# Turning round the order of heads and channels on the partitions of a linear attention stage

## What is computed

```
ms = concatenate([qkv, agg], axis=1).reshape(B, 64, 24, 4096)      # 64 heads: 8 q, 8 k, 8 v channels each
q, k = relu(q), relu(k);  v = v with a column of ones
kv  = einsum('bgnd,bgne->bgde', k, v)                               # per head 8 x 9
out = einsum('bgnd,bgde->bgne', q, kv)
out = out[..., :-1] / (out[..., -1:] + 1e-15)
x   = x + conv1x1(out, w_proj)                                      # 512 -> 256 channels
```

## Time and profile before

| | |
|---|---|
| three runs | 8548.59, 8554.9, 8555.37 us; median 8554.9 |
| the profiled execution | 8550.38 us, its span 8548.7 us |
| TensorE busy over the span | 93% |
| VectorE, GpSimd, ScalarE busy | 66%, 52%, 42% |
| linear attention, first load to last store | 2558.87 to about 3308 us |
| TensorE's granted clock, mean | 0.979 of 2.4 GHz |

### The profile page before, as it was taken

How to read it: one execution, slowest core, us unless ns; L and a number is a source line. 1 busy time by engine, 2 the same in 40 slices (tenths; PEclk the granted TensorE clock), 3 DMA queues, 4 the chain that set the end, 5 groups by cost and what they waited for, 6 DMA issues and landing times. The chain is left out here.

```text
span 8548.7 us, 155575 instructions
## 1 busy us (share of the span) xinstructions
PE 7935.8 (93%) x55794; PEld 6737.4 (79%) x55794; DVE 5657.7 (66%) x8857; ACT 3583.2 (42%) x7004; POOL 4479.1 (52%) x1996
## 2 busy tenths in 40 slices
PE   5999998899996996999999999999999999969999
PEld 4777776799995774888888888888888888857777
DVE  5666664344442556998888888989988898851110
ACT  3555555333322332555445454455554555531110
POOL 3555551033330001777778777777777877841111
PEclk9999999999998998999999999999999999989999
DMA  3111115755555541000000000000000000022221
GB/s 136 56 62 57 62 51 188 243 144 142 145 138 209 205 179 54 13 18 13 17 12 13 18 13 17 12 13 18 18 13 11 13 18 18 6 72 61 63 57 53
DMA packets 613257, 567.80 MB, mean 66 GB/s; under 512 B 464085, under 2 KB 481621, under 8 KB 610374
## 3 DMA queue, kind: packets, MB, share of 16 engines
q1 hardware_dynamic: 578246, 455.11, 18.2%
q0 software_dynamic: 33856, 96.69, 3.1%
q10 hardware_dynamic: 576, 8.39, 0.2%
HBM read 366.33 MB, written 193.76 MB: 66 GB/s over the span
## 5 line engine op out<-in xcount | busy, mean ns | idle before, releaser
L1824 POOL TENSOR_TENSOR e_ev<-e_se,e_v 128x2048 f32<-128x2048 f32 (+1 forms) x896 | 3307.9, 3713 | 940.6 <-ACT e_se L1787 940.6
L1787 ACT ACTIVATE e_se<-e_stage 128x512 f32<-128x512 f32 x3136 | 1870.1, 598 | 2074.4 <-PE e_stage L1654 2044.4
L1915 DVE SCALAR_TENSOR_TENSOR e_stage<-e_k,e_rl,e_qp 128x512 f32<-128x512 f32 x3136 | 2299.1, 746 | 330.8 <-ACT e_se L1787 296.7
L1661 PE MATMUL e_pv_sum<-e_ident,e_ev 128*128 128x128 f32 x12544 | 1872.5, 273 | 35.7 <-issue 35.2
L1661 PE MATMUL e_pe_sum<-e_ident,e_se 128*128 128x128 f32 x12544 | 1879.7, 272 | 12.4 <-ACT e_se L1787 12.2
L1661 PEld LDWEIGHTS e_pe_sum<-e_ident,e_se 128*128 128x128 f32 x12544 | 1557.8, 140 | 241.5 <-ACT e_se L1787 16.8
L1661 PEld LDWEIGHTS e_pv_sum<-e_ident,e_ev 128*128 128x128 f32 x12544 | 1485.5, 141 | 266.2 <-issue 213.6
L1654 PE MATMUL e_stage<-e_top,e_minus 128*128 128x512 f32 x3136 | 1509.5, 481 | 51.8 <-DVE e_stage L1915 47.2
L403 POOL TENSOR_TENSOR a_pr<-a_pr,a_rden 128x480 f32<-128x480 f32 x512 | 495.1, 990 | 587.4 <-DVE a_rden L636 587.4
L903 POOL DMA_DIRECT2D agg<-c_ot x384 | 334.6, 874 | 887.5 <-DVE c_ot L962 776.7
L1654 PEld LDWEIGHTS e_stage<-e_top,e_minus 128*128 128x128 f32 x3136 | 595.8, 190 | 108.3 <-DVE e_stage L1915 81.2
(11 more groups left out here) (160 smaller groups left out, 11911.3 us busy)
## 6 DMA issues: line engine op xcount, KB each, us to landing
qkv<-b_ot SPq DMA_DIRECT2D x120, 512.0 KB, 5.9
c_xt<-qkv SPq DMA_DIRECT2D x384, 160.0 KB, 3.8
agg<-c_ot POOLq DMA_DIRECT2D x384, 160.0 KB, 2.5
a_xb<-in_x SPq DMA_DIRECT2D x24, 768.0 KB, 5.0
a_xr<-in_x SPq DMA_DIRECT2D x32, 512.0 KB, 3.8
x<-a_xr SPq DMA_DIRECT2D x32, 512.0 KB, 2.8
b_xc<-x SPq DMA_DIRECT2D x32, 512.0 KB, 6.1
d_xr<-x POOLq DMA_DIRECT2D x32, 512.0 KB, 7.8
```

The costliest lines, as they stand in the source:

```text
L1661: last = nc.tensor.matmul(acc[:, c * PART:(c + 1) * PART], lhsT=src[:, c * PART:(c + 1) * PART], rhs=ident[:], is_transpose=True, start=j ...
L1787: nc.scalar.activation(se[(t * K2 + o) % NSE][:, i], stage[:, bank_of(t, j), :], ACT.Exp)\
L1824: nc.gpsimd.tensor_tensor(split(ev[(t * NG2 + g) % NEV][:, 0:size]), split(se[(t * K2 + o) % NSE][:, i:i + size]), window(v[h], h, u, o, i ...
L1915: nc.vector.scalar_tensor_tensor(rows(stage[:, bank_of(t, j), :]), win, rl[:, h, o:o + 1], rows(qp[:]), ALU.add, ALU.mult).then_inc(multip ...
```

## The change

The DRAM pattern of the loads gets the head as its outer and the channel as its inner dimension, so that partition p holds channel p % 8 of head p // 8. Mask, mask column, denominators and products follow; the rows of the projection weights need no reordering any more. The patterns on the chip's side of the loads stay, 128 partitions by the run's pixels, and so do sizes, counts and waits.

```
-            return bass.AP(tensor=one.tensor, offset=one.offset, ap=[[BLKPX, G8], [3 * GPX, TG], [1, (last - first) * WW]])
+            return bass.AP(tensor=one.tensor, offset=one.offset, ap=[[3 * GPX, TG], [BLKPX, G8], [1, (last - first) * WW]])
...
-                nc.vector.tensor_scalar(kvm[b % 2][:, st, PART:ONE], hm[:, 0:TG], pkv[:, PART:PART + 1], None, ALU.mult)\
+                nc.vector.tensor_scalar(kvm[b % 2][:, st, PART:ONE], hm[:].rearrange("p (g i) -> p g i", i=G8)[:, :, 0], pkv[:, PART:PART + 1], None, ALU.mult)\
...
-                    last = nc.vector.tensor_tensor(attp[i % 2][:, sub].rearrange("p s (i g) -> p s i g", g=TG),
-                                                   ratios[:, h, :, 0:PART].rearrange("p s (i g) -> p s i g", g=TG),
-                                                   den[i % 2][:, sub].rearrange("p s (o g) -> p s o g", o=1)
-                                                   .to_broadcast([PART, SPB, G8, TG]), ALU.mult)
+                    last = nc.vector.tensor_tensor(attp[i % 2][:, sub].rearrange("p s (g i) -> p s g i", g=TG),
+                                                   ratios[:, h, :, 0:PART].rearrange("p s (g i) -> p s g i", g=TG),
+                                                   den[i % 2][:, sub].rearrange("p s (g o) -> p s g o", o=1)
+                                                   .to_broadcast([PART, SPB, TG, G8]), ALU.mult)
...
 def head_mask():
-    h = np.arange(PART) % TG
+    h = np.arange(PART) // G8
     return (h[:, None] == h[None]).astype(np.float32)
-
-
-def head_channels():
-
-    return np.arange(ST * PART).reshape(ST, TG, G8).transpose(0, 2, 1).reshape(-1)
...
-        "L1_w_proj_t": a["L1_conv_w_proj"].reshape(C, ST * PART).T[head_channels()],
+        "L1_w_proj_t": a["L1_conv_w_proj"].reshape(C, ST * PART).T,
```

## The result

The kernel with the change takes 8509.9 us (median of 6 runs, 8495.7 to 8518.3) against 8550.3 before (6 runs, 8547.6 to 8555.4): a ratio of 0.995, with a 95% interval of 0.9937 to 0.9963, or 40 us less. The prediction was 8489, in a range of 8476 to 8516. The direction and the place came as forecast, and 16 engines work where 8 did; the rate of these 16 did not, so the gain is 61% of the 66 us, and the case that came is the one called partial gain. The profiled execution happens to be the fastest of the six, 8495.7 us with a span of 8493.9.

The account below looks back on a forecast made before the run. Linear attention's lead-in and image 0 were taken as bound by loads using half the DMA engines; 54 + 12 = 66 us off 8550.4 gives 8484, plus 4.5 for the median of three, 8489, range 8476 to 8516.

Parts of the forecast that it names:

- partial gain: Rival for the linear attention's loads: 16 engines run but share something, about 260 GB/s, 41 us less, 8514 us; chance 0.10.
- the 32 chunks: Lead-in, image 0: copies of keys every 1.94 us once data is there, last one 23.7 us earlier.
- VectorE's new pattern: Multiply by the reciprocal, each denominator now repeated 8 times in a row: no cost, 418 ns a call.
- image 0 gives 12 us: Image 0's attention steps: waits for queries end, 13.6 us over the stall-free time, 12 us saved.
- TensorE's clock: Image 0: 1.6 us kept back because the clock may have dropped during the clips.
- The step that failed: Load rate in the lead-in: 333 to 431 GB/s instead of 205, with 333 costing 2 us.
- the queries: End of lead-in: 26.8 MB in by 2623 to 2641, clips unstalled, first ACT copy of attention at 2643.1 instead of 2697.73.
- the 54 booked: Lead-in up to the first copy of attention: 54.6 us saved together, put at 54.
- the first data: Start of lead-in: TensorE starts at 2570 instead of 2576.86, 6.9 us earlier.
- the rule of ports: Loads: four neighbouring partitions share one of 16 ports, so engines could meet on 8; set aside as today's pattern runs full rate.
- The rival without a change: Loads stay at 205 GB/s through another limit or another choice of engines; 8555 us, chance 0.11.
- The slower one: Rival: the order of DRAM reads costs, loads fall under 205 GB/s, at 150 the time is 8611 us; chance 0.03.

Follow-up runs that it names:

- halves: Kernel with the change, each load issued as two of 8 heads on 64 partitions, slowest DRAM dimension 8 again; ratio 1.0001 to the kernel before.
- kinds: Kernel with the change, channel groups ordered by kind on the host, qkv and agg laid out for one-stride loads, right data; 8478.7 us, ratio 0.9917.
- rows160k: Kernel with the change, loads reading 128 rows at one stride of 160 KB (other data); 396 GB/s, no time given.
- near2d: Kernel with the change, loads of 16 by 8 rows, the 16 lying 36 KB apart instead of 480 KB (other data); 269 GB/s, no time given.
- again: Kernel with the change, rerun unchanged; 268 GB/s, 109.4 us from first load to first copy of attention, no total time given.

## Why the prediction was right, and where it was off

Right by the runs: that half of the DMA engines stood idle because the slowest dimension was 8 (halves); that only the lead-in and image 0 gain, and that images 1 and 2 are TensorE's; that the 32 chunks then go at 1.94 us each, with the pauses gone (copies of keys 1 and 32 lie 61.7 us apart, 62.8 by the sum); that VectorE's new pattern costs nothing (418 ns); that image 0 gives 12 us (165.7 to 153.45 in one execution and 152.8 in the other); that some of it goes to TensorE's clock (0.67 and 0.90 granted in the two stretches about its start); that later stages shift by the whole.

The number lies inside the range by luck more than by the forecast. The forecast's own range ended at 8506; it was widened to 8516 to take in the partial case, which had 0.10, and 8509.9 lies in what was added. The 8489 also stood on the median of three runs of the kernel before, 8554.9; from the 8550.3 of six the same sum gives 8484.

The step that failed is the rate, and with it the queries. The sum took the rate to lie between 333 and 431 GB/s, and said that 333 would cost 2 us. It was 301 in one execution and 268 in the other. The 26.8 MB ahead of the last clip then need 89 or 100 us instead of 62 to 80, and the first copy of attention came 98.4 and 109.4 us after the first load where the sum had 84. The lead-in gave 40.5 and 29.5 us for the 54 booked. The smaller part is in the first data: 14.2 us to TensorE's start for the 11.1 booked.

The lower bound of the rate was set wrongly. I read 333 GB/s in the projection as what a split by 16 groups yields, although loads with another pattern ran in the same stretches, and I took the row as a floor. A loss of the same kind was in it: with kinds, where those stores have one stride too, the DMA share of 1390 to 1650 us falls from 0.85 to 0.75 for the same 283 to 285 GB/s, and a store of qkv lands in 4.4 us (the median) by the list of issues, where it took 5.9. The stretch in before, the stretch in kinds, and the issues of kinds:

```profile
1390.00:1650.00 260.00, 253.37 (x1105) 207.53 (x1103) 90.26 (x117) 109.79 (x162) 0.00 (x0) 0.99 0.85 283
```

```profile
1390.00:1650.00 260.00, 249.97 (x1093) 204.75 (x1091) 89.62 (x116) 108.81 (x159) 0.00 (x0) 0.99 0.75 285
```

```profile
qkv<-b_ot SPq DMA_DIRECT2D x120, 512.0 KB, 4.4
```

The prediction also set aside the rule of ports because 8 engines on blocks of 16 partitions ran at full rate. That row is true, and halves repeats it with blocks of 8, but it does not carry over to 16 engines: 8 engines lose nothing, 16 lose a quarter to a third of 396 GB/s. The rival "partial gain" named the right thing, engines that share something, with 260 GB/s and 8514 us; it deserved more than 0.10. Its own sum, 41 us less, is what the medians show. The rival without a change falls by the share of 1.05. The slower one falls by the rate, which is over 205 GB/s in both executions; that distance in DRAM costs nothing is shown by rows160k and near2d.

That the medians lie 40 us apart and the profiled executions 54.8 is for the larger part the scatter of that same rate, by the two profiles of one program. More than that the runs do not show: the kernel after ran within 23 us over six runs and the kernel before within 8, but thirteen others of the kernel before lie within 16, and four of near2d, at 269 GB/s, within 6.

## What to carry to other kernels

A DMA share that sits at a round fraction, with a high rate for each busy engine, was a count of engines here, and the outer dimension of the DRAM pattern is where to look; turning two dimensions round gave 40 us. A share of 1 is not the end of it: GB/s divided by the share tells whether the engines run at full pace, and laying the tensor out so that a load of 128 partitions has one stride gave another 31 us. Price such a change at the rate of a row with the same pattern that is saturated by that pattern alone, and where no row has it, take the range from the idle rate up.

## What was not expected of the hardware

- The same program loads at 301 GB/s in one execution and at 268 in another (packets of 201 and 226 ns), while one stride over 128 partitions had 396 to 397 GB/s and 144 ns in each of its three runs, one profile each.
- 32 groups of 4 rows ran at 396 GB/s and 16 groups of 8 at 269, with the same 128 partitions, sizes and number of DMAs.
- After the change SP issued the first 19 loads 0.6 to 1.1 us apart, and the twentieth was the first to be held up for long, where before the change it was the seventh. In again the thirteenth took 1.32 us. The lines of the kernel after:

```profile
2569.75 0.65 SPq L1121 DMA_DIRECT2D d_kt<-qkv  x1
2570.44 3.19 SPq L1121 DMA_DIRECT2D d_vt<-qkv  x1
```
